# Row statistics moved into the attention stage, the weighing split between two engines, and the feed-forward stage's step put in another order

## The reference

```python
def bitlinear(x, w, g):
    xn = rmsnorm(x, g)
    xq = xn + jax.lax.stop_gradient(act_quant(xn) - xn)     # 127 / max|xn| per row, rounded
    wq = w + jax.lax.stop_gradient(weight_quant(w) - w)
    return jnp.einsum('bsd,fd->bsf', xq, wq)
h = jax.nn.gelu(bitlinear(x, w1, g1), approximate=False)    # 192 -> 768
return bitlinear(h, w2, g2)                                 # 768 -> 192
...
h = h + _L0_attn_ref(_layernorm(h, axis=-1), ...)
h = h + _L0_ffn_ref(_layernorm(h, axis=-1), ...)
```

## Time and profile before

| | us |
|---|---|
| median of 3 runs | 1894.72 |
| lowest, highest | 1888.71, 1895.52 |
| the profiled execution, its own time | 1889.4 |
| its span, first to last instruction | 1887.7 |

### The profile page before, as it was taken

One profiled execution on the slowest core, in us unless ns is written; L12 is line 12 of the kernel. 1 busy time (PEld: TensorE's weight loads), 2 busy tenths in 40 slices (PEclk: granted clock), 3 DMA queues, 4 the chain that ended last, 5 costly groups with the idle time before them and its releaser, 6 DMA issues.

```text
span 1887.7 us, 50796 instructions
## 1 busy us (share of the span) xinstructions
PE 1579.8 (84%) x16574; PEld 1297.6 (69%) x16574; DVE 1364.8 (72%) x3151; ACT 1283.7 (68%) x1958; POOL 1089.7 (58%) x1503
## 2 busy tenths in 40 slices
PE   0539999999999999999999999999466666666666
PEld 0427788888888888888888888887345555555555
DVE  3636676767767676767676767676389999999996
ACT  1226666766767676767676666665288888888887
POOL 5035555555555555555555555554177777777775
PEclk9869999999999999999999999999666666666665
DMA  8674666665657565756565666660000000000000
GB/s 102 141 127 59 95 87 96 86 99 83 103 79 104 83 99 83 99 88 94 89 94 91 91 93 88 94 87 25 17 16 21 21 21 22 22 22 22 22 22 26
DMA packets 159967, 132.96 MB, mean 70 GB/s; under 512 B 32558, under 2 KB 151040, under 8 KB 159808
## 3 DMA queue, kind: packets, MB, share of 16 engines
q1 hardware_dynamic: 159168, 131.00, 44.4%
q0 software_dynamic: 768, 1.57, 0.5%
HBM read 118.32 MB, written 11.91 MB: 69 GB/s over the span
## 4 chain that ended last, share of the span: by engine, by line
PE 66%; DVE 15%; issue 7%; SPq 3%; ACT 3%; DMA 3%; POOL 1%; DVEq 1%; ACTq 0%; POOLq 0%
PE ps L1092 20%; PE ps L1176 8%; PE ps L1259 7%; PE ps L1250 7%; PE ps L1206 4%; DVE ff_st L860 4%; PE ps L1238 3%; PE ps L1232 3%; PE ps L1211 3%; PE ps L1336 2%; PE ps L1355 2%; DVE xpix L841 2%; PE ps L1167 2%; DVE xpix L853 1%; PE ps L1157 1%
## 5 line engine op out<-in xcount | busy, mean ns | idle before, releaser
L1092 PE MATMUL ps<-w_eff,pix 118*112 118x193 f32 (+1 forms) x2048 | 408.4, 337 | 25.0 <-ACT pix L909 24.3
L927 ACT ACTIVATE probs<-ps,isw 116x688 f32<-116x688 f32 x384 | 299.2, 831 | 171.6 <-PE ps L1238 171.6
L527 POOL TENSOR_TENSOR xpix<-probs,g_b 112x192 f32<-112x192 f32 (+1 forms) x512 | 296.5, 609 | 109.1 <-ACT probs L1044 99.7
L741 DVE TENSOR_REDUCE nmax<-ps 116x12 bf16<-116x1344 f32 (+2 forms) x192 | 299.6, 1560 | 80.2 <-PE ps L1211 77.7
L452 POOL TENSOR_TENSOR xsq<-xsq 118x784 f32<-118x784 f32 (+2 forms) x192 | 221.8, 1155 | 218.5 <-ACT xsq L920 208.4
L1092 PEld LDWEIGHTS ps<-w_eff,pix 118*112 118x112 f32 (+1 forms) x2048 | 309.8, 167 | 52.4 <-issue 18.9
L472 POOL TENSOR_SCALAR_AFFINE_SELECT probs<-probs 116x464 f32<-116x464 f32 x384 | 268.2, 717 | 46.5 <-ACT probs L927 31.0
L909 ACT ACTIVATE pix<-xpix 118x896 f32<-118x896 f32 (+1 forms) x128 | 198.4, 1552 | 104.9 <-DMA xpix<-in_x 56.0
L457 POOL TENSOR_TENSOR front_st<-front_st,expo 128x2 f32<-128x2 f32 x64 | 45.0, 703 | 235.2 <-DVE front_st L693 221.2
L1336 PE MATMUL ps<-w1t,xpix 96*112 96x384 f16 (+1 forms) x512 | 160.7, 488 | 14.6 <-ACT xpix L1035 13.3
L685 DVE TENSOR_SCALAR front_st<-ps 112x1 f32<-112x1 f32 (+1 forms) x128 | 18.3, 151 | 213.8 <-PE ps L1157 202.4
(11 more groups left out here) (161 smaller groups left out, 3363.3 us busy)
## 6 DMA issues: line engine op xcount, KB each, us to landing
xpix<-in_x SPq DMA_DIRECT2D x192, 196.0 KB
xpix<-in_x SPq DMA_DIRECT2D x192, 195.1 KB
rden<-den_rows SPq DMA_DIRECT2D x256, 85.5 KB, 2.1
out<-xpix SPq DMA_DIRECT2D x64, 87.0 KB
out<-xpix SPq DMA_DIRECT2D x64, 84.0 KB
xpix<-in_x SPq DMA_DIRECT2D x128, 34.1 KB
xpix<-in_x SPq DMA_DIRECT2D x128, 34.0 KB
den<-o_sb SPq DMA_DIRECT2D x256, 2.7 KB
```

The lines of the kernel that those rows point to most:

```text
L527: last = nc.gpsimd.tensor_tensor(v2[0:P, b, tile, cols], gel[0:P, b, tile, cols], g2_b[0:P, cols], ALU.mult)
L741: V.tensor_reduce(dst, src, AX_X, ALU.max, negate=True).then_inc(s_mx, 1)
L927: A(probs[0:TB, g, 2 * e:2 * e + 2, :], ps[0:TB, 4 + 2 * e:6 + 2 * e, 0:SK], ACT.Exp, scale=isw[0:TB, 7:8]).then_inc(s_p, 1)
L1092: last = MM(ps_tok[tile][0:P, :], src, w_eff[0:HI, o, :], start=(o == 0), stop=(o == OFFS - 1))
```

## The change

1. The statistics of the second layernorm leave the feed-forward stage. A new function `measure(n-1)` stands at the end of each DVE step of the attention stage: statistics, aggregation, the variance term, a copy of the mean to `mean2`, the centred and weighted rows (into `v1`, which is now the same memory as `tok_t`), and their largest absolute value into `peak`. POOL gets one small power operation per image for it (`row_roots`). After the last image DVE makes all scales of the first quantiser at once, for 128 columns.
2. In the feed-forward step DVE only centres the rows again (`centre`) and quantises them.
3. Weighing of the gelu output: tile 0 goes to DVE (`weigh`), tile 1 stays on POOL. Second quantiser: tile 0 stays on ACT, tile 1 goes to DVE (`quantise_second`). The mean-square term goes to POOL; the square's scale takes in the division by 768.
4. The order within a step is new on all four engines; `turn_second` and the copy after it are one step later than before.

```diff
+            def measure(n):
...
+                dve.wait_ge(s_h2, n + 1)
+                apart(dve)
+                for tile, P in enumerate((TA, TB)):
+                    last = V.bn_stats(ln_st[0:P, 20 + 6 * tile:26 + 6 * tile], h_all[0:P, hcols(n, tile)])
+                chain(last, 1)
...
+                    last = V.bn_aggr(ln_st[0:P, 34 + 2 * tile:36 + 2 * tile], ln_st[0:P, 20 + 6 * tile:26 + 6 * tile])
+                chain(last, 2)
+                after(dve, s_rms, n)
+                V.tensor_scalar(ln_st[:, 32:34], ln_st[:, 35:38:2], 1.0 + EPS_RMS,
+                                EPS_LN * EPS_RMS, ALU.mult, ALU.add).then_inc(s_var2, 1)
+                V.tensor_copy(mean2[:, bass.ds(n * 2, 2)], ln_st[:, 34:38:2])
...
+                    last = V.scalar_tensor_tensor(v1[0:P, tile, :], h_all[0:P, hcols(n, tile)],
+                                                  ln_st[0:P, 34 + 2 * tile:35 + 2 * tile], g1_b[0:P, :],
+                                                  ALU.subtract, ALU.mult)
+                chain(last, 3)
...
+                    last = V.tensor_reduce(peak[0:P, bass.ds(n * 2 + tile, 1)], v1[0:P, tile, :], AX_X, ALU.max,
+                                           apply_absolute_value=True)
+                last.then_inc(s_peak, 1)
@@ DVE, attention step @@
                 if new:
                     maxima(n + 1, 2)
+                if prev:
+                    measure(n - 1)
@@ DVE, between the stages @@
+            dve.wait_ge(s_peak, IMAGES)
+            dve.wait_ge(s_rms, IMAGES)
+            link(V.tensor_tensor(peak[:, :], rms[:, :], peak[:, :], ALU.mult))
+            link(V.tensor_scalar(peak[:, :], peak[:, :], 1e-5, None, ALU.max))
+            link(V.reciprocal(inv_peak[:, :], peak[:, :]))
+            V.tensor_scalar(step1[:, :], peak[:, :], isw[:, 4:5], None, ALU.mult)
+            link(V.scalar_tensor_tensor(scale1[:, :], inv_peak[:, :], 127.0, rms[:, :], ALU.mult, ALU.mult))
@@ DVE, feed-forward step @@
+                if new:
+                    centre(i + 1)
+                    quantise_first(i + 1)
+                if last_:
+                    final(i - 3, 1 - b)
                 if mid:
+                    weigh(i - 1, 1 - b)
+                    peaks(i - 1, 1 - b)
+                    second_scales(i - 1, 1 - b)
+                    quantise_second(i - 1, 1 - b)
@@ POOL, feed-forward step @@
+            def weight(n, b):
+                after(pool, f_q2[1], n - 1)
+                pool.wait_ge(f_g, 2 * n + 2)
...
+            with pool.Fori(1, PAIRS) as t:
                 for b in range(2):
+                    weight(2 * t + b, b)
+                    gelu_roots(2 * t + b, b)
@@ ACT, feed-forward step @@
+            def quantise(n, b):
+                act.wait_ge(f_sc, n + 1)
+                after(act, f_t2, n)
+                A(q2[0:TA, 0, :], v2[0:TA, b, 0, :], ACT.Copy, bias=MAGIC16,
+                  scale=ff_st[0:TA, b, 38:39]).then_inc(f_q2[0], 1)
...
+            def ffn_step(i, b, new=True, mid=True, turned=True):
                 if new:
+                    copy_first(i + 1)
+                if turned:
+                    copy_second(i - 2)
+                if new:
+                    gelus(i + 1, 1 - b)
+                    gelu_squares(i + 1, 1 - b)
                 if mid:
+                    quantise(i - 1, 1 - b)
@@ PE, feed-forward step @@
             def turn_second(n):
-                pe.wait_ge(f_q2, n + 1)
                 after(pe, f_t2s, n)
                 for tile, P in enumerate((TA, TB)):
+                    pe.wait_ge(f_q2[tile], n + 1)
...
-            def ffn_step(i, new=True, mid=True, last_=True):
+            def ffn_step(i, new=True, turned=True):
+                if turned:
+                    turn_second(i - 2)
                 if new:
                     turn_first(i + 1)
-                if last_:
+                    ffn_first(i + 1)
+                if turned:
                     ffn_second(i - 2)
-                if new:
-                    ffn_first(i + 1)
-                if mid:
-                    turn_second(i - 1)
```

More of the change, by code:

```diff
@@ L569, in _ @@
             step(V.memset(nmax[:, :, :], 0.0))
+            for filled in (mean2, rms, peak):
+                step(V.memset(filled[:, :], 1.0))
             dve.wait_ge(s_const, 32)
@@ new lines, in centre, with quantise_first @@
+            def centre(n):
+                after(dve, f_q1, n)
+                for tile, P in enumerate((TA, TB)):
+                    ins = V.scalar_tensor_tensor(v1[0:P, tile, :], h_all[0:P, hcols(n, tile)],
+                                                 mean2[0:P, bass.ds(n * 2 + tile, 1)], g1_b[0:P, :],
+                                                 ALU.subtract, ALU.mult)
+                ins.then_inc(f_v1, 1)
+            def quantise_first(n):
+                dve.wait_ge(f_v1, n + 1)
+                after(dve, f_t1, n)
+                for tile, P in enumerate((TA, TB)):
+                    ins = V.tensor_scalar(q1[0:P, tile, :], v1[0:P, tile, :], scale1[0:P, bass.ds(n * 2 + tile, 1)],
+                                          MAGIC16, ALU.mult, ALU.add)
+                ins.then_inc(f_q1, 1)
@@ new lines, in final, with weigh @@
+            def final(n, b):
+                dve.wait_ge(f_m2, n + 1)
+                after(dve, f_out, 32 * n)
+                for tile, P in enumerate((TA, TB)):
+                    end = V.scalar_tensor_tensor(y[0:P, tile, :], ps[0:P, 1, tile * 256:tile * 256 + DIM],
+                                                 ff_st[0:P, b, 42 + tile:43 + tile], h_all[0:P, hcols(n, tile)],
+                                                 ALU.mult, ALU.add)
+                end.then_inc(f_y, 1)
+            def weigh(n, b):
+                for tile, P in ((0, TA),):
+                    after(dve, f_q2[tile], n - 1)
+                    dve.wait_ge(f_g, 2 * n + tile + 1)
+                    V.tensor_tensor(v2[0:P, b, tile, :], gel[0:P, b, tile, :], g2_b[0:P, :],
+                                    ALU.mult).then_inc(f_v2[tile], 1)
@@ new lines, in quantise, with copy_first @@
+            def quantise(n, b):
[3 more added lines that the diff above has]
+                  scale=ff_st[0:TA, b, 38:39]).then_inc(f_q2[0], 1)
+            def copy_first(m):
+                act.wait_ge(f_t1, m + 1)
+                after(act, f_m1, 2 * m)
+                for tile, P in enumerate((TA, TB)):
+                    src = bank16(0, 4 * TB, F16).rearrange("p (t c k) -> p t c k", t=2, c=2)
+                    ins = A(q1T[0:HALF, tile, :, 0:P], src[0:HALF, tile, :, 0:P], ACT.Copy, bias=-MAGIC16)
+                ins.then_inc(f_t1s, 1)
@@ new lines, in copy_second, with gelus @@
+            def copy_second(j):
+                act.wait_ge(f_t2, j + 1)
+                after(act, f_m2, j)
+                for tile, P in enumerate((TA, TB)):
+                    src = bank16(6 + tile, NCH * TB, F16).rearrange("p (c k) -> p c k", c=NCH)
+                    ins = A(q2T[:, tile, :, 0:P], src[:, :, 0:P], ACT.Copy, bias=-MAGIC16)
+                ins.then_inc(f_t2s, 1)
+            def gelus(m, b):
+                for tile in range(2):
+                    after(act, f_v2[tile], m - 1)
+                for tile, P in enumerate((TA, TB)):
+                    act.wait_ge(f_m1, 2 * m + tile + 1)
+                    A(gel[0:P, b, tile, :].rearrange("p (c d) -> p c d", c=2),
+                      ps[0:P, 2 + 2 * tile:4 + 2 * tile, 0:HIDDEN // 2], ACT.Gelu,
+                      scale=step1[0:P, bass.ds(m * 2 + tile, 1)]).then_inc(f_g, 1)
@@ L1072, in _ @@
             ffn_step(IMAGES, 0, new=False)
+            ffn_step(IMAGES + 1, 1, new=False, mid=False)
         @block.tensor
```

248 lines of the change are left out of this document (98 added, 150 removed).

## The result

The changed kernel took 1937.18 us (median of 4 runs, 1931.36 to 1940.59); the kernel before, beside it, 1893.51 us. The ratio is 1.0231 with a 95% interval of 1.0199 to 1.0263: slower by 2.3%, 44 us. The prediction was 1926 us, slower by 1.7%, in a range of 1895 to 1948 us.

A forecast was written before the change was run, and what follows sets the result against it. It took PE to bound the attention stage and, after the change, a PE-ACT ring the feed-forward stage; 0 + 1.8 + 28.3 + 4.1 = +34 us on 1889.4 gave 1923.6, median put at 1926 us, range 1895 to 1948.

The forecast's parts named there:

- What bounds the kernel: Attention stage bound by PE, busy 299.21 of 300 us; feed-forward stage by DVE, 92% busy, at 7.92 us a step.
- PE's clock: Feed-forward stage: the 12 transposes get the faster clock in about half the steps, taking 8.72 us to 8.45; first product stays slow.
- measure hidden, 0: Attention stage: the moved statistics, 2.7 us, fit DVE's 3.1 us wait for PE's sums and add 0.
- Between the stages, +1.8: Between attention and feed-forward: last image's statistics, five operations on 128 columns and centring take 5.5 us against 3.72.
- DVE's own step, 7.35 us: Feed-forward stage: by DVE alone the step would fall from 7.92 to 7.35 us, staying ahead of PE and ACT.
- rival of a DVE-bound step: Feed-forward stage: DVE sets the step after all at 7.35 us, giving 1857 to 1862 us; chance 0.11.
- The ring, 8.45 us: Feed-forward stage: PE's 16 transposes and ACT's whole list run in series, 8.45 us a step, +28.3 us over 63 steps.
- Behind the last copy, +4.1: End of the feed-forward stage: the last image's chain takes some 24 us against 19.8.
- The sum: Whole kernel: 0 + 1.8 + 28.3 + 4.1 = +34 us on the profiled execution's 1889.4 us, giving 1923.6.
- late `measure`: Attention stage: statistics of 3.4 us make DVE late by 0.3 us in each of 61 steps, 1942 to 1945 us; chance 0.08.
- faster clock: Feed-forward stage: the ring closes but PE gets its fast clock more often, 8.0 us a step, 1897 to 1901 us; chance 0.11.

The follow-up runs named there:

- before_filled: The kernel before with 14 matmuls of 128 columns, result unread, at the end of PE's feed-forward step: 1879.01 us, ratio 0.9927 to the kernel before.
- both: The changed kernel with PE's 4 new-image transposes ahead of the 12, and tile 1 ahead of tile 0 within the 12: 1818.64 us, ratio 0.9617 to the kernel before.
- old_order: The changed kernel's work and split between engines, with PE and ACT in the order of the kernel before: 1824.76 us, ratio 0.9657 to the kernel before.
- first_ahead: The changed kernel with two PE calls exchanged, the new image's 4 transposes ahead of the middle image's 12: 1826.71 us, ratio 0.9651 to the kernel before.
- tile1_first: The changed kernel with the 12 transposes done for tile 1 first, then tile 0: 1874.26 us, ratio 0.9892 to the kernel before.
- quant_dve: The changed kernel with the second quantiser of tile 0 moved from ACT to DVE: 1844.32 us, ratio 0.9753 to the kernel before.
- pe_filled: The changed kernel with 14 matmuls of 128 columns, result unread, behind the second product of each feed-forward step: 1862.61 us, ratio 0.9863 to the kernel before.
- weigh_pool: The changed kernel with the weighing of tile 0 moved from DVE back to POOL: 1934.13 us, ratio 1.0221 to the kernel before.
- both_filled: The changed kernel with both PE exchanges and 10 matmuls, result unread, behind the second product: 1818.22 us, ratio 0.9612 to the kernel before.

## Why the prediction was right, point by point

- **What bounds the kernel.** Right for the attention stage. The feed-forward stage was read as DVE's, from 92% busy; before_filled shows that 0.2 us of its step went with PE's clock, so DVE was not the bound of every step.
- **measure hidden, 0.** Right: 0.4 us between the means, inside the scatter. It ran in 2.6 us (for the last image 1366.67 to 1369.25; 2.7 was said), in a wait of 3.1.
- **Between the stages, +1.8.** Measured +1.9. The reciprocal on 128 columns took 0.95 us (up to 1 was said), the others 0.23 to 0.29. Timeline of the changed kernel:

```profile
1369.29 0.29 DVE L855 TENSOR_TENSOR peak<-rms,peak 128x128 f32<-128x128 f32 x1
1369.61 0.23 DVE L856 TENSOR_SCALAR peak<-peak 128x128 f32<-128x128 f32 x1
1369.87 0.95 DVE L857 RECIPROCAL inv_peak<-peak 128x128 f32<-128x128 f32 x1
1370.86 0.29 DVE L858 TENSOR_SCALAR step<-peak,isw 128x128 f32<-128x128 f32 x1
```

- **DVE's own step, 7.35 us.** Wrong, too high: in `both`, where DVE sets it, a step is 6.70 us. The step that failed is the sum from before's mean step, in three terms. By the starts of DVE's lines (means of the steps from 1420 to 1780 us, before against `both`): what left, L823 to the start of L853 without the wait for PE, took 2.99 us in the loop and not the 2.50 of the first image, and `centre` takes 0.88 for 0.77, so 2.1 went and not 1.73. In it is L835, the mean-square term, which went to POOL and had no price. The maxima, the scales and the first quantiser take 1.85, 0.92 and 0.60 us where they took 1.92, 1.50 and 0.77: 0.8 less for 0.3. Against that `weigh` takes 1.29 for 1.10; `quantise_second` takes its 0.55. Some of the first two terms are delays. Groups by form, the kernel before and then the changed kernel, against the earlier trace rows:

```profile
L831 DVE TENSOR_SCALAR ff_st<-ff_st 128x2 f32<-128x2 f32 x50 | 21.1, 423 | 1.7
...
L900 DVE TENSOR_TENSOR xpix<-probs,g_b 112x768 f32<-112x768 f32 x51 | 64.1, 1256 | 0.0
L926 DVE TENSOR_SCALAR probs<-xpix,ff_st 116x768 f16<-116x768 f32 x52 | 32.3, 620 | 1.8
L916 DVE TENSOR_SCALAR ff_st<-ff_st 128x2 f32<-128x2 f32 x52 | 8.8, 170 | 1.8
```

  L916 takes 0.170 us where L867 took 0.483 on four columns. It goes by where POOL's work falls: the same line takes 0.463 in old_order. The one large delay left is of the kind that the Trainium skill's GPSIMD Engine Reference (section 8, Key points) names, contention of POOL with a DVE instruction that has two SBUF inputs: `weigh` takes 1.256 us on average beside POOL's pieces. The trace agrees: in old_order POOL is idle during 51 of the 63 weighings after the first, and each of these takes 0.94 to 0.95. View of that line alone in old_order (minimum, median, maximum in ns):

```profile
L900 DVE TENSOR_TENSOR xpix<-probs,g_b x64: 937/944/1349, 1375.3 to 1808.0; 112x768 f32<-112x768 f32 x64
```

  DVE's step did not carry the forecast, but it priced the rival of a DVE-bound step, which would have been 1815 to 1820 us, not 1857.
- **The ring, 8.45 us.** This was the step that decided, and it was right: the waits and the chain show it, the five kernels in which it is opened or shortened (first_ahead, tile1_first, both, quant_dve, old_order) are all faster, and pe_filled shows that a higher clock alone does not make up for them. The 61 full turns, from the third copy to the 64th, took 8.58 us each:

```profile
1385.58 0.58 ACT L1089 ACTIVATE xpix<-ps 96x224 f16<-96x224 f16 x2
...
1909.12 0.60 ACT L1089 ACTIVATE xpix<-ps 96x224 f16<-96x224 f16 x2 [1.86 <-PE ps L1393]
```

  At the low clock 8.93 against my 8.72, at the high clock 7.06 against my 7.2. The 0.2 us missing at the low clock are mostly in one term: from the copy's start to the second tile's gelu is 3.68 in place of 3.50; the squares' 1.65 and the quantiser's 0.98 are as priced, the transposes with the handover to the copy 1.82 in place of 1.79. In part the mean came out by compensation: the slow turn was priced 0.21 us too low, and the clock took 0.35 off it (8.93 to 8.58) where 0.27 was taken.
- **PE's clock.** As taken: the 12 transposes took 0.76 to 0.78 us in 27 of the 61 turns and 1.30 to 1.32 in 28, and the first product 2.80 or 2.81 in 57. The Trainium skill (TensorE: Matmul & The Clock Gate, "HAM oscillation") has pauses between stretches of matmuls bring the low clock. The trace agrees in the main: 1.00 from 600 to 900 us, where PE does not pause, and 0.60 here, though the section's example is a longer wait for data than any pause here (at most 2.3 us from 1420 to 1860 us). That two pauses weigh more than one, 0.60 against 0.65 in the same stretch of before, fits, but no run separates it. What I did not see is how strongly it reacts in the other direction: every kernel that opened or shortened the ring also raised the clock, to 0.69 to 0.81.
- **Behind the last copy, +4.1.** Measured +2.9: DVE's weighing, maxima and scales of the last image took 3.7 us (1921.23 to 1924.94), and 5 was said.
- **The sum.** +34 us on the profiled execution, measured +47.5 on this pair of profiles: 36.3 against 28.3 from the steps (0.13 us each for 61), 6.4 against 0 from the attention stage, which is scatter in the main, 1.9 against 1.8, 2.9 against 4.1. By medians +44 against +31 to 34.
- **Rivals.** The DVE-bound step did not come (weigh_pool: DVE busier, the step the same). The late `measure` did not come. The faster clock did not come in the changed kernel; pe_filled shows that it would have given 1863 us, even less than the 1897 to 1901 that I gave it.

## What to carry to other kernels

Before the order of a software pipeline is changed, walk once around each pair of engines: if the last instruction of one engine's step is what the first of the other's step waits for, and that one's next is what the first engine's next step waits for, the two steps run in series, and a third engine's work does not count as long as it fits beside them: here 1.5 us more of DVE a step changed nothing. Work that is ready early (here the new image's 4 transposes) goes ahead of work that waits for the end of a step, not behind it. When the busy shares fall or stay while the step grows, look for such a ring in the waits, not for a cost. And when work is moved off an engine, look at its busy time afterwards: a neighbour's work can lengthen what stayed by more than what went.

## What the runs showed that was not expected

- Adding 14 useless matmuls to each step made the changed kernel 3.8% faster (1937 to 1863 us) and the kernel before 0.7% (ratio 0.9927), through a granted clock of 0.90 and 0.87 in place of 0.60 and 0.65. Where DVE set the step it gave nothing (both_filled), though there the clock rose by 0.03 to 0.07 only.
- The clock and the ring reinforce each other: two calls exchanged raised the granted clock from 0.60 to 0.80.
- Taking DVE's weighing (1.25 us) away made DVE busier, because one operation on two columns went from 0.16 to 1.96 us beside POOL's weighing (weigh_pool).
- The attention stage, in ten kernels with the same program in it, differs by several us between profiled executions (1177 to 1186 us between the first and the last inversion), so that a difference of 6 us there between two profiles is no finding.
